# Causal attention on one Trainium2 core: weighted sums and denominators by one full-width matmul with values and ones side by side

## What is computed

```python
xn = layernorm(x, g1)
q = xn @ Wq.T
kv = xn @ Wkv.T
k, v = (kv[..., :DIM_HEAD], kv[..., DIM_HEAD:])
q = q.reshape(b, n, HEADS, DIM_HEAD).transpose(0, 2, 1, 3)
q = q * SCALE
q, k = (l2norm(q), l2norm(k))
srt = np.sqrt(SCALE).astype(np.float32)
q, k = (q * srt, k * srt)
sim = jnp.einsum('bhid,bjd->bhij', q, k)
sim = jnp.where(causal_mask, max_neg, sim)
attn = jax.nn.softmax(sim.astype(jnp.float32), axis=-1).astype(sim.dtype)
out = jnp.einsum('bhij,bjd->bhid', attn, v)
out = out.transpose(0, 2, 1, 3).reshape(b, n, HEADS * DIM_HEAD)
out = out @ Wout.T
return layernorm(out, g2)
```

## Time and profile before

| | us |
|---|---|
| median of 3 runs | 3709.29 (3705.96 to 3709.39) |
| profiled execution, its own time | 3702.01 |
| its span | 3700.3 |
| granted TensorE clock, mean | 0.947 |
| TensorE matmul busy | 3169.0 (86%) |
| ScalarE busy | 1979.0 (53%) |
| VectorE busy | 1799.3 (49%) |
| GpSimd busy | 1151.5 (31%) |
| causal phase, from the first ones of GpSimd to the last logarithm of denominators | 1978.1 to 2868.0 |

### The profile page before, as it was taken

How to read it: one execution, slowest core, us unless ns; L and a number is a source line. 1 busy time by engine, 2 the same in 40 slices (tenths; PEclk the granted TensorE clock), 3 DMA queues, 4 the chain that set the end, 5 groups by cost and what they waited for, 6 DMA issues and landing times. The chain is left out here.

```text
span 3700.3 us, 44165 instructions
## 1 busy us (share of the span) xinstructions
PE 3169.0 (86%) x12438; PEld 1675.1 (45%) x12438; DVE 1799.3 (49%) x2639; ACT 1979.0 (53%) x3736; POOL 1151.5 (31%) x954
## 2 busy tenths in 40 slices
PE   3777777769999999996667999999999769999997
PEld 1222222236777777763223444444444534444443
DVE  3877777754555555556994433433333321111110
ACT  3555555525555555553555777777777433323322
POOL 2666666631222222224663333333333000000000
PEclk9888888879999999998888999999999989999999
DMA  5333333320000000000110000000000210000001
GB/s 205 112 109 108 108 108 108 108 64 17 16 20 15 20 15 20 15 16 29 51 43 26 13 17 13 13 17 13 17 13 12 105 72 17 17 20 23 17 17 60
DMA packets 100808, 167.55 MB, mean 45 GB/s; under 512 B 11520, under 2 KB 42384, under 8 KB 100240
## 3 DMA queue, kind: packets, MB, share of 16 engines
q1 hardware_dynamic: 100752, 166.88, 13.4%
HBM read 81.57 MB, written 4.72 MB: 23 GB/s over the span
## 5 line engine op out<-in xcount | busy, mean ns | idle before, releaser
L1359 POOL TENSOR_TENSOR d_pr<-d_pr,d_keep 128x512 f32<-128x512 f32 x256 | 320.1, 1271 | 564.9 <-ACT d_pr L1517 564.9
L282 PE MATMUL a_py<-a_prod,consts 128*128 128x512 f32 x512 | 308.6, 693 | 78.8 <-DVE a_prod L535 46.2
L776 POOL TENSOR_TENSOR b_pn<-b_e,b_inv 128x616 f32<-128x616 f32 x128 | 161.3, 1260 | 671.7 <-DVE b_inv L955 671.7
L262 POOL TENSOR_TENSOR a_bx<-a_bcopy,a_drive_u 128x512 f32<-128x512 f32 x256 | 320.3, 1265 | 55.0 <-DVE a_state L529 54.6
L529 DVE TENSOR_TENSOR_SCAN a_state<-a_decay,a_bx 128x512 f32<-128x512 f32 x256 | 310.8, 1214 | 1.4 <-POOL a_bx L262 1.4
L882 ACT ACTIVATE b_yy<-b_py,y_bias 128x154 f32<-128x154 f32 x512 | 169.8, 385 | 248.0 <-PE b_py L822 247.8
L458 ACT ACTIVATE a_decay<-a_delta,neg_a 128x508 f32<-128x508 f32 x256 | 174.9, 684 | 177.0 <-DVE a_state L529 175.5
L1912 PE MATMUL f_ph<-f_hb,wb 128*128 128x512 f32 x512 | 232.8, 599 | 6.3 <-ACT f_hb L1947 6.3
L1912 PE MATMUL f_ph<-f_ha,wb 128*128 128x512 f32 x512 | 229.0, 596 | 2.3 <-DVE f_ha L1976 2.3
L535 DVE TENSOR_TENSOR a_prod<-a_state,a_pc 128x512 f32<-128x512 f32 x256 | 175.8, 687 | 101.6 <-issue 90.5
L282 PEld LDWEIGHTS a_py<-a_prod,consts 128*128 128x128 f32 x512 | 102.3, 219 | 219.4 <-DVE a_prod L535 124.0
(11 more groups left out here) (282 smaller groups left out, 6535.0 us busy)
## 6 DMA issues: line engine op xcount, KB each, us to landing
a_bcopy<-rows SPq DMA_DIRECT2D x256, 256.0 KB, 3.3
wb<-in_wb SPq DMA_DIRECT2D x1, 6714.0 KB, 33.5
x<-in_x SPq DMA_DIRECT2D x1, 4096.0 KB
a_xf<-x SPq DMA_DIRECT2D x16, 256.0 KB, 3.8
a_xt<-x SPq DMA_DIRECT2D x16, 256.0 KB, 2.3
x<-a_xo SPq DMA_DIRECT2D x16, 256.0 KB, 3.7
b_xf<-x SPq DMA_DIRECT2D x32, 128.0 KB, 2.0
b_xt<-x SPq DMA_DIRECT2D x32, 128.0 KB, 2.0
```

The source lines that it names most:

```text
L262: gp.tensor_tensor(bx[:, k % 4, :], bcopy[:, k % 4, :], drive_u[:, p, :], ALU.mult).then_inc(*bxt.step("bx"))
L282: mm(py[:], S["ident"][:], prod[:, j % 4, :], start=j == 0, stop=j == SLOTS - 1).then_inc(*pey.step("y"))
L1359: gp.tensor_tensor(half, half, keep[:].unsqueeze(1).to_broadcast([128, QP, SEQ]), ALU.mult).then_inc(*gmt.step(f"m{odd}"))
```

## The change

`vv` gets three blocks of 64 columns for each sequence: ones, values, ones, all filled with ones at the phase's start, and the middle one written with the values for each group. For the even heads blocks 1 and 2 (values, ones) are the weights, for the odd heads blocks 0 and 1 (ones, values). Each of the two matmuls now uses 128 columns of weights and fills a whole bank: the even heads' sums lie in partitions 0 to 63 of bank 0 and their denominators in 64 to 127, the odd heads' denominators in 0 to 63 of bank 1 and their sums in 64 to 127. `pattn` has both banks, `pden` is gone. ScalarE's logarithm and VectorE's product, which covered both parities in one operation, are done for each parity by itself.

```diff
-        vv = sb("vv", [128, 2, NB, DH])
-        ones = sb("ones", [128, DH])
+        vv = sb("vv", [128, 2, NB, 3, DH])
...
-        pattn = ps("pattn")
-        pden = ps("pden")
+        pattn = ps("pattn", 1024)
...
-                gp.memset(ones[:], 1.0).then_inc(*made.step("ones"))
+                gp.memset(vv[:], 1.0).then_inc(*made.step("ones"))
...
-                    for bank, w in ((pattn, vv[:, p, b, :]), (pden, ones[:])):
-                        for odd in range(2):
-                            op = mm(bank[64 * odd:64 * odd + 64, :], w, pr[:, j % 2, odd, :], start=True, stop=True,
-                                    skip_group_check=True)
+                    for odd in range(2):
+                        w = vv[:, p, b, 1 - odd:3 - odd, :].rearrange("p i d -> p (i d)")
+                        op = mm(pattn[:, 512 * odd:512 * (odd + 1)], w, pr[:, j % 2, odd, :], start=True, stop=True)
                     op.then_inc(*pea.step("a"))
...
-                            A(den[:], pden[:], ACT.Ln).then_inc(*sdt.step("ln"))
+                            for odd in range(2):
+                                op = A(den[64 * odd:64 * odd + 64, :],
+                                       pattn[64 - 64 * odd:128 - 64 * odd, 512 * odd:512 * (odd + 1)], ACT.Ln)
+                            op.then_inc(*sdt.step("ln"))
...
-                            V.tensor_copy(vv[:, q, :, :], pn[:, 0:NB * DH].rearrange("p (b d) -> p b d", b=NB)
+                            V.tensor_copy(vv[:, q, :, 1, :], pn[:, 0:NB * DH].rearrange("p (b d) -> p b d", b=NB)
                                           ).then_inc(*vf.step("v"))
...
-                            V.tensor_tensor(attn[:, pu, QP * hh:QP * (hh + 1), SEQ * b:SEQ * (b + 1)],
-                                            pattn[:].rearrange("p (i t) -> p i t", i=QP),
-                                            den[:].rearrange("p (i t) -> p i t", i=QP), ALU.mult
-                                            ).then_inc(*vat.step("n"))
+                            for odd in range(2):
+                                half = slice(64 * odd, 64 * odd + 64)
+                                op = V.tensor_tensor(
+                                    attn[half, pu, QP * hh:QP * (hh + 1), SEQ * b:SEQ * (b + 1)],
+                                    pattn[half, 512 * odd:512 * (odd + 1)].rearrange("p (i t) -> p i t", i=QP),
+                                    den[half, :].rearrange("p (i t) -> p i t", i=QP), ALU.mult)
+                            op.then_inc(*vat.step("n"))
```

## The result

| | before | after |
|---|---|---|
| median of the runs, us | 3707.87 | 3747.28 |
| lowest to highest | 3705.96 to 3709.39 | 3743.84 to 3747.88 |
| span of the profiled execution, us | 3700.3 | 3741.7 |
| ScalarE busy, us | 1979.0 | 2057.0 |
| VectorE busy, us | 1799.3 | 1890.0 |

The ratio is 1.0105, 95% interval 1.0087 to 1.0122: 39.4 us slower. I forecast slower by 11.4 us and a range up to 3738; the measured time lies above it. The sign and every wait that the forecast named are there, but the step is more than three times as long.

What follows compares the result with a forecast made beforehand. Each group was taken as half ScalarE-paced, half TensorE-paced. Terms +0.73, +0.37 and -0.70 gave +0.40 us a group, +11.4 in all after about 1 off for end groups: 3720 us, range 3687 to 3738.

Steps and rivals of the forecast that it cites:

- ScalarE's half, up to the lengths of i3: Two added logarithms, 2 x 0.49, less 0.25 us slack, delay the length matmul of a group's piece i3: +0.73 us a group.
- TensorE's wait for `xo`: Variance matmul waits for VectorE's output product to free its bank, 0.27, plus 0.10 for openly loaded weights: +0.37 us a group.
- TensorE's half, j3 and j0: In the TensorE-paced half of a group, units j3 and j0 save 0.35 us each: -0.70 us a group.
- D: Rival: full-width weights not hidden, each pass 0.10 us dearer, +1.1 a group, 3743 us; chance 0.05 together with another rival.
- The bound: Each causal-phase group has a ScalarE-paced and a TensorE-paced half, meeting at i3's length matmul, where ScalarE has 0.25 us slack.
- TensorE's 0.35 per unit: Full-width matmuls for sums and denominators avoid changes of array shape: 2.07 us before, 1.72 after, 0.35 less per unit.
- A2: Rival: all of TensorE's 44.8 us saving over 128 units comes through, 3664 us; chance 0.05.
- ScalarE's second logarithm, 0.49: Splitting the denominators' logarithm into two of 64x512 adds 0.49 us a unit; bounds 0 and 0.61.
- Rival C: Dearer split: second logarithm 0.61 us, second product 0.69, +0.73 us a group in all, 3732 us; chance 0.07.
- VectorE's second product, 0.60: Splitting VectorE's product into two 64x512 adds 0.60 us (bounds 0 and 0.69), costing only where someone waits behind it.
- TensorE's wait of 1.3 us before the lengths of i2: Expected sign: TensorE's wait before i2's length matmul grows from 0.50 to about 1.3 us (0.50 + 0.49 + 0.35).
- The count of cover: ScalarE's waits behind the denominators of j3 (1.61 us) and j0 (0.47) absorb the added 0.49 in TensorE's half.

## Why the prediction was right in kind and wrong in size

| term, us a group | forecast | measured |
|---|---|---|
| ScalarE's half, up to the lengths of i3 | +0.73 | 2 x 0.73 - 0.25 = +1.21 |
| TensorE's wait for `xo` | +0.37 | +0.54 (undone alone) |
| TensorE's half, j3 and j0 | -0.70 | -0.64 (made alone) |
| sum | +0.40 | +1.11; the group grew by 1.16 |

The sum of the measured terms leaves 0.05 us a group open. Of the rivals D, with 3743, comes nearest to the measured 3747, but by luck: its dearer passes aren't there.

**The bound.** Right. From the scores of j2 (2608.81) to the lengths of i3 (2623.28) there are now 14.47 us. Before, the scores of j2 were:

```profile
2610.33 1.13 PE L1375 MATMUL d_pscore<-d_qn,d_kn 64*128 64x512 f32 x4
```

and the lengths of i3 at 2623.58, 13.25 later. This is +1.22, the table's first row. In the second half TensorE has no wait but that for `xo`. The prediction names one wait of ScalarE in its half; there is another, of 0.28 us for VectorE before the logarithm of `roots` in slot 4 (it starts at 2614.52 before and 2613.00 after). It stands ahead of both units' denominators and is as long in both kernels, so that it gave no cover.

**TensorE's 0.35 per unit.** Right for three units. For j0 it is less, 0.29: its sums take 1.77 behind the short value matmuls. A2, that all of it comes through, is refuted by the run with the matmuls alone: -0.64 and not -1.4. So is D: the sums of a unit take 1.71, not 1.72 + 4 x 0.10 = 2.12.

**ScalarE's second logarithm, 0.49.** This is the step that failed. I priced it by two exponentials on all 128 partitions that follow each other in the same place, and took 0.61 as the upper end. It starts 0.61 behind the first, and the first itself starts 0.12 late, which I had not counted at all: 0.73. The row with 77 partitions only told that half the partitions don't halve the time, and that held. Rival C had the 0.61 and lacked the 0.12 before it. Twice 0.24 a group goes straight into the path: 0.48 x 31 = 15 us, as the two kernels with logarithms in one place give back (0.50 and 0.52 a group).

**VectorE's second product, 0.60.** The same error, by the row of `xo` behind one product: 0.82. It made the bank wait 0.54 and not 0.37, 5 us over the phase.

**The start of the phase.** I took 1 us off for the first and last groups; it is 4 us on top until the first `xo`. The longer waits are there from the first group on (2.12 us before its lengths of i2, in the kernel before 1.08), and within a group `xo` itself comes 2.28 later behind the exponentials of j2 (24.20 - 9.99 against 23.43 - 11.50).

**TensorE's wait of 1.3 us before the lengths of i2.** Measured 1.35, but not by my sum: 0.50 and ScalarE's 0.73, and only 0.1 for TensorE's own saving of 0.35. Of the rest 0.14 went where ScalarE's square held back the lengths of i1, and 0.1 where the centering matmul now meets VectorE's sum (14.60 - 13.99 = 0.61 to the next scores, before 0.52, 2615.71 to 2616.23).

**The count of cover.** Right in its outcome. ScalarE's wait behind j3's denominators shrank from 1.61 to 0.98 us. Behind those of j0 the cover was smaller than put down: the 0.47 stand before the exponentials of j2, but the square of i1 comes ahead of them and had only 0.23 of its own. It now ends at 9.38 + 0.58 = 9.96, and the lengths of i1 start 0.14 late. The group doesn't grow by it: the exponentials of j2 still start 1.18 behind their scores (9.99 - 8.81; before 11.50 - 10.33 = 1.17), and TensorE's loss falls into its wait of 1.35.

## What to carry to other kernels

A busy share of 97% did not mean that TensorE's savings come through: in a group of 27 us they did where no other engine's result was awaited, and nowhere else. An operation of 512 columns split by partitions into halves took about its full time once more here on ScalarE and VectorE (0.73 and 0.82 us), on ScalarE 0.24 of it for overlaps lost where the first partition read or written changed. A layout that saves TensorE 0.35 us but splits two operations behind it pays only if those lie off the path. Price an added operation by a row with the same change of place, or take one without any overlap.

## What the runs showed of the hardware that I had not expected

In these traces ScalarE overlaps two operations by some 0.1 us where both the input (per memory) and the output start at the partition where the last one did, and not where one of them moved from 0 to 64 or back: 0.48 against 0.60 from start to start for 512 columns. The change and five of the experiments' kernels show it, the last of them forecast from the rule; that a write alone is enough is shown only where the operation also crosses from one half to the other. VectorE's reciprocal takes 3.35 us for 512 columns, on 64 partitions as on 128, nearly five times its product of 0.69. Two column halves of a matmul ran side by side at about the pace of one full-width pass: four half-width passes took 0.91 us, two full-width ones 0.86. So full width saved only what comes with the change of shape, 0.35 us a unit.
